# One graph layer's sums: the one-hot cast goes to GpSimd, five bins as pairs, ScalarE weighs five bins

## The chip, the cores and the metric

The kernel runs on one core of a Trainium2 chip. The metric is the device time in microseconds of one execution; three executions of the kernel before took 3258.47, 3259.68 and 3259.81 us, median 3259.68. The engines are TensorE (PE, with its weight loads as PEld), VectorE (DVE), ScalarE (ACT), GpSimd (POOL) and SyncE (SP), which issues the transfers.

## The reference

Two graph attention layers over 6250 nodes of 128 channels and 200000 edges, each followed by a residual and a layer norm. The change lies in the first:

```python
hij = concatenate([h[src], h[dst]], -1)
exp_e = exp(leaky_relu(hij @ w, 0.2) @ a)
denom = segment_sum(exp_e, src)
out = segment_sum(h[src] * exp_e / denom[src], dst)
x = layernorm(x + out)
```

What follows concerns the last two lines: rows of x divided by denom, gathered by source, weighed by exp_e, and summed by target.

## The kernel before, in words

Nodes stand in 49 blocks of 128 (node = block and lane). Earlier stages sort the edges into bins, one for each pair of a target block n and a source block b, at most 128 edges each, and leave for every bin the score of its edges (`e0`, one column of 128), the source lanes of its edges (in memory, `src_rows`) and the target lanes (`k.SL`). Then `layer0_sums` runs (from about 1318 to 2183 us of the profile). After it come `norm_and_project` and the second layer, `layer1`, which the change leaves alone, but which has instructions of the same kinds.

`layer0_sums` first divides x by denom and splits it into three bf16 parts (`parts`); VectorE and ScalarE share that work, which reaches into the first block's turns. The main loop has R = 343 turns, t = 0 to 342: seven turns for each target block n, and in each turn GX = 7 bins. A turn is made of these steps:

- SyncE fetches the source lanes, the same for all partitions (`got`, a ring of LOADS buffers).
- `make` (VectorE, L922): compares them with the partition's number: 128x896 bf16, seven one-hot matrices.
- `gather` (TensorE, L1009): 7 x 3 bf16 matmuls select the source rows into PSUM (`gps`, two buffers).
- `weigh` (VectorE, L930): the first SPLIT = 4 bins from PSUM times their scores, into `msg`.
- `weigh_late` (ScalarE, L1064): the other three bins, one instruction each, with the same result.
- `take_high` (ScalarE, L1070): copies the four bins, rounded to fp32r, into the first half of `halves`; `take_low` (VectorE, L936): subtracts that from the four bins and puts the remainder into the second half. A bin is then a pair of 128 columns that one fp32r matmul of 256 columns multiplies at once.
- `find_lanes` (VectorE, L847, a helper that other stages use too): one-hot matrices of the target lanes, 128x896 bf16 (`lane`).
- `widen` (ScalarE, L1055): casts them to fp32r (`lane_wide`).
- `add_up` (TensorE): the three late bins as full fp32 matmuls, two records each (L1020), then the four pairs (L1025), all into `acc`.

Once in seven turns, for the block that has been finished, VectorE's `take` adds the two halves of `acc` into S (a reduction, L941), GpSimd adds S to X (L995), and VectorE measures the rows for the layer norm (`measure` L946, `average` L950). ScalarE's `stage` lays out a block's target lanes.

The order on each queue is written out by hand. VectorE in turn t: make(t+2), weigh(t), find_lanes(t+1), take_low(t), and what is due for the block. ScalarE: weigh_late(t), take_high(t), widen(t+1). TensorE: gather(t+1), add_up(t). The rings `lane`, `lane_wide`, `msg` and `halves` have two buffers, `hot` has three.

Of the kernel before, what the change touches and what calls it, by code (L numbers as in the profile page):

```python
# [851 lines left out]
def layer0_sums(nc, k, parts, xs, den, src_rows, e0, X, S, mean_var):  # L852
    NB, PER = NBK, NBK // GX
    R = NB * PER
    RING, LOADS, SPLIT = 3, 4, 4
    BY_SCALAR = (2, 4, 6)
    F32R = mybir.dt.float32r
    with Stage(nc) as ctx:
        def sb(name, shape, dt=F32):
            return ctx.enter_context(nc.sbuf_tensor(f"l0_{name}", shape, dt))  # L860
# [11 lines left out]
        lane, lane_wide = sb("lane", [P, 2, GX, P], BF16), sb("lane_wide", [P, 2, GX, P], F32R)  # L872
        lane_pairs = sb("lane_pairs", [P, 2, NB, 2], BF16)
        msg, halves = sb("messages", [P, 2, GX, C]), sb("message_halves", [P, 2, SPLIT, 2, C], F32R)
        stats = sb("stats", [P, 2, 6])
        gps = ps("gathered", [P, 2, 1024])
        acc = ps("acc", [P, 2, 512])
# [11 lines left out]
        with nc.Block() as block:  # L889
# [10 lines left out]
            def _(dve):  # L900
# [24 lines left out]
                def weigh(t):  # L925
                    n, g = divmod(t, PER)
                    dve.wait_ge(s["gathered"], t + 1)
                    if t >= 2:
                        dve.wait_ge(s["low"], t - 1)
                    nc.vector.tensor_tensor(msg[:, t % 2, 0:SPLIT], gps[:, t % 2, 0:SPLIT * P].rearrange("p (i c) -> p i c", i=SPLIT),  # L930
                                            e0[:, n, g * GX:g * GX + SPLIT].unsqueeze(2).to_broadcast([P, SPLIT, C]), ALU.mult
                                            ).then_inc(s["messages"], 1)

                def take_low(t):
                    dve.wait_ge(s["high"], t + 1)
                    nc.vector.tensor_tensor(halves[:, t % 2, :, 1, :], msg[:, t % 2, 0:SPLIT], halves[:, t % 2, :, 0, :], ALU.subtract  # L936
                                            ).then_inc(s["low"], 1)

                def take(n):
                    dve.wait_ge(s["added"], (n + 1) * PER)  # L940
                    nc.vector.tensor_reduce(S[:, n, :], acc[:, n % 2, 0:2 * C].rearrange("p (q c) -> p c q", q=2), AX.X, ALU.add  # L941
                                            ).then_inc(s["taken"], 1)

                def measure(n):
                    dve.wait_ge(s["summed"], n + 1)
# [5 lines left out]

                def find_lanes(t):
                    n, g = divmod(t, PER)
                    if t >= 2:
                        dve.wait_ge(s["lane_wide"], t - 1)
                    if g == 0:
                        dve.wait_ge(s["staged"], n + 1)
                    compare_lanes(nc, k, lane[:, t % 2], lane_pairs[:, n % 2, g * GX:(g + 1) * GX, :]).then_inc(s["lane"], 1)

                ch.link(nc.vector.tensor_scalar(den, den, 1.1754944e-38, None, ALU.max))  # L960
                ch.link(nc.vector.reciprocal(rden[:], den))
                scale(0)
                scale(1)
                part_rest(0)
                for t in range(-2, R):
                    c = t + 3
                    if c + 1 < PER and c + 1 not in BY_SCALAR:
                        scale(c + 1)
                    if c < PER:
                        part_rest(c)  # L970
# [16 lines left out]
                take(NB - 1)  # L987
                measure(NB - 1)
                average(NB - 1)

            @block.gpsimd
            def _(pool):
                for n in range(NB):
                    pool.wait_ge(s["taken"], n + 1)
                    nc.gpsimd.tensor_tensor(X[:, n, :], X[:, n, :], S[:, n, :], ALU.add).then_inc(s["summed"], 1)  # L995

            @block.tensor
            def _(pe):
                def gather(t):
                    n, g = divmod(t, PER)  # L1000
# [12 lines left out]
                def add_up(t):  # L1013
                    n, g = divmod(t, PER)
                    pe.wait_ge(s["late_messages"], t + 1)
                    pe.wait_ge(s["lane_wide"], t + 1)
                    if g == 0 and n >= 2:
                        pe.wait_ge(s["taken"], n - 1)
                    for i in range(SPLIT, GX):
                        nc.tensor.matmul(acc[:, n % 2, 0:C], lane_wide[:, t % 2, i, :].bitcast(F32), msg[:, t % 2, i, :],  # L1020
                                         start=(g == 0 and i == SPLIT), stop=False, skip_group_check=True)
                    pe.wait_ge(s["low"], t + 1)
                    for i in range(SPLIT):
                        last = g == PER - 1 and i == SPLIT - 1
                        ins = nc.tensor.matmul(acc[:, n % 2, 0:2 * C], lane_wide[:, t % 2, i, :],  # L1025
                                               halves[:, t % 2, i].rearrange("p h c -> p (h c)"), start=False, stop=last,
                                               skip_group_check=True)
                    ins.then_inc(s["added"], 1)

                for t in range(-1, R):  # L1030
                    if t + 1 < R:
                        gather(t + 1)
                    if t >= 0:
                        add_up(t)

            @block.scalar
            def _(act):
# [13 lines left out]
                def widen(t):  # L1051
                    act.wait_ge(s["lane"], t + 1)
                    if t >= 2:
                        act.wait_ge(s["added"], t - 1)
                    nc.scalar.copy(lane_wide[:, t % 2], lane[:, t % 2]).then_inc(s["lane_wide"], 1)  # L1055

                def weigh_late(t):
                    n, g = divmod(t, PER)
                    act.wait_ge(s["gathered"], t + 1)
                    if t >= 2:  # L1060
                        act.wait_ge(s["added"], t - 1)
                    for i in range(SPLIT, GX):
                        b = g * GX + i
                        ins = nc.scalar.activation(msg[:, t % 2, i, :], gps[:, t % 2, i * P:(i + 1) * P], ACT.Copy,  # L1064
                                                   scale=e0[:, n, b:b + 1])
# [17 lines left out]
                part_middle(0)  # L1083
                part_high(2)
                part_middle(1)
                widen(0)
                for t in range(R):
                    c = t + 3
# [8 lines left out]
                    if t + 1 < R:  # L1097
                        widen(t + 1)
                    if t % PER == 3 and t // PER + 1 < NB:
                        stage(t // PER + 1)  # L1100

# [1424 lines left out]
```

## Time and profile before

The profiled execution spans 3274.5 us from the first to the last instruction, 14.8 us (0.45%) above the median of the times. The trace gives no other time of its own.

| | busy us | share of the span |
|---|---|---|
| PE | 3060.7 | 93% |
| PEld | 2792.8 | 85% |
| DVE | 3045.9 | 93% |
| ACT | 2750.1 | 84% |
| POOL | 155.0 | 5% |

An engine's busy time is the union of its instructions; neighbouring instructions of one engine overlap a little. The end of a matmul is modelled, so for TensorE the distance between starts is read. "Idle before" is the engine's idle time ahead of a group, with what ended it. A duration on GpSimd holds what the instruction waited for after its start.

### The profile page before, as it was taken

The page shows a single profiled execution, that of the slowest core. Times are in us where ns is not written, and L with a number is a line of the kernel's source. Part 1 is how long each engine was busy: PE and PEld are TensorE (multiplying, and loading weights), DVE is VectorE, ACT ScalarE, POOL GpSimd, SP SyncE. Part 2 cuts the span into 40 slices and gives each one's busy share as a digit, 9 for nine tenths or more (in the row PEclk, how much of TensorE's full clock was granted, in tenths as well). Part 3 has the DMA queues.
Part 4 walks back from the last instruction along what each step waited for, and adds up shares of the span by engine and source line. Part 5 has one row for each costly group of instructions (what it writes and reads, how often), then busy time and mean ns, then how long its engine had stood idle before and what let it go on. Part 6 is the DMA issues. An engine that isn't in the chain of part 4 may idle for free. (4 is left out here: it accounts for less than half of the span.)

```text
span 3274.5 us, 101508 instructions
## 1 busy us (share of the span) xinstructions
PE 3060.7 (93%) x40072; PEld 2792.8 (85%) x40072; DVE 3045.9 (93%) x4921; ACT 2750.1 (84%) x6946; POOL 155.0 (5%) x249
## 2 busy tenths in 40 slices
PE   5777699999999999699999999989999999999996
PEld 4666677778777877699999999988999999999994
DVE  8999889999999997799999999989999999999997
ACT  6988888888888885799999999987888888888887
POOL 0000000000000000000000000000111111111110
PEclk9989899999999997799999999999999999999998
DMA  3000022222222222234333333334455545554541
GB/s 66 13 14 11 23 98 93 87 93 94 93 87 93 94 86 48 65 96 97 97 97 96 97 96 97 97 93 137 161 163 160 164 161 163 161 163 161 162 151 41
DMA packets 173823, 333.06 MB, mean 102 GB/s; under 512 B 54876, under 2 KB 109616, under 8 KB 173264
## 3 DMA queue, kind: packets, MB, share of 16 engines
q1 hardware_dynamic: 170996, 323.30, 32.5%
q8 instruction: 322, 5.28, 0.7%
q10 hardware_dynamic: 2348, 3.20, 0.4%
q14 instruction: 157, 1.29, 0.1%
HBM read 320.77 MB, written 5.66 MB: 100 GB/s over the span
## 5 line engine op out<-in xcount | busy, mean ns | idle before, releaser
L1009 PE MATMUL l_gathered<-xp,l_src_onehot 128*128 128x128 bf16 x7203 | 467.0, 221 | 11.2 <-DVE l_src_onehot L922 11.2
L1436 PE MATMUL l_gathered<-hp,l_onehot 128*128 128x128 bf16 x7203 | 458.5, 219 | 0.0
L704 PE MATMUL sc_z<-sc_onehot,pq 128*128 128x256 f32 (+1 forms) x2450 | 429.4, 298 | 23.3 <-DVE sc_leaky L617 18.3
L1009 PEld LDWEIGHTS l_gathered<-xp,l_src_onehot 128*128 128x128 bf16 x7203 | 407.9, 99 | 26.3 <-DVE l_src_onehot L922 11.7
L788 ACT ACTIVATE sc_leaky<-sc_z 128x1024 f32<-128x1024 f32 (+3 forms) x325 | 309.8, 953 | 143.3 <-PE sc_z L708 140.5
L617 DVE SCALAR_TENSOR_TENSOR sc_leaky<-sc_z,sc_leaky 128x1024 f32<-128x1024 f32 (+3 forms) x325 | 370.1, 1139 | 60.0 <-ACT sc_leaky L788 52.5
L847 DVE TENSOR_TENSOR l_lane<-iota_b,l_lane_pairs 128x896 bf16<-128x896 bf16 x686 | 421.0, 614 | 0.0
L1436 PEld LDWEIGHTS l_gathered<-hp,l_onehot 128*128 128x128 bf16 x7203 | 406.1, 98 | 0.4
L708 PE MATMUL sc_z<-sc_onehot,pq 128*128 128x256 f32 (+1 forms) x2450 | 400.9, 286 | 0.0
L1450 PE MATMUL l_acc<-e,l_lane_wide 128*128 128x132 f32 x2744 | 385.5, 283 | 0.3 <-ACT e L1514 0.3
L704 PEld LDWEIGHTS sc_z<-sc_onehot,pq 128*128 128x128 f32 x2450 | 344.6, 196 | 35.9 <-issue 34.5
L708 PEld LDWEIGHTS sc_z<-sc_onehot,pq 128*128 128x128 f32 x2450 | 344.1, 195 | 0.0
L1343 DVE TENSOR_TENSOR e<-l_gathered,l_weight 128x768 f32<-128x768 f32 x343 | 325.5, 949 | 12.7 <-issue 9.1
L1450 PEld LDWEIGHTS l_acc<-e,l_lane_wide 128*128 128x128 f32 x2744 | 336.2, 190 | 0.8 <-ACT e L1514 0.5
L1503 ACT CAST l_lane_wide<-l_lane 128x896 fp32r<-128x896 bf16 x343 | 329.0, 959 | 0.0
L1055 ACT CAST l_lane_wide<-l_lane 128x896 fp32r<-128x896 bf16 x343 | 322.2, 939 | 4.0 <-DVE l_lane L847 4.0
L1508 ACT CAST l_message_halves<-e 128x396 fp32r<-128x396 f32 x343 | 179.1, 522 | 158.8 <-DVE e L1343 155.4
L1020 PE MATMUL l_acc<-l_messages,l_lane_wide 128*128 128x128 f32 x2058 | 306.0, 285 | 5.7 <-ACT l_messages L1064 5.7
L1064 ACT ACTIVATE l_messages<-l_gathered,e 128x128 f32<-128x128 f32 x1029 | 301.5, 363 | 0.0
L609 DVE TENSOR_SCALAR sc_onehot<-placed,part 128x1536 fp32r<-128x1536 uint8 (+1 forms) x300 | 298.9, 997 | 0.1
L936 DVE TENSOR_TENSOR l_message_halves<-l_messages,l_message_halves 128x512 fp32r<-128x512 f32 x343 | 237.5, 692 | 53.0 <-ACT l_message_halves L1070 48.2
L1514 ACT ACTIVATE e<-l_gathered,l_weight 128x32 f32<-128x32 f32 x1372 | 280.4, 286 | 0.0
(246 smaller groups left out, 6107.4 us busy)
## 6 DMA issues: line engine op xcount, KB each, us to landing
rows_got<-edge_rows_wide SPq DMA_DIRECT2D x338, 448.0 KB, 3.7
l_got<-edge_rows_src SPq DMA_DIRECT2D x343, 224.0 KB, 3.2
placed<-edge_rows SPq DMA_DIRECT2D x144, 512.0 KB, 3.7
out_dram<-X SPq DMA_DIRECT2D x12, 256.0 KB
S<-edge_rows_wide SPq DMA_DIRECT2D x5, 448.0 KB, 8.4
edge_rows<-e SPq DMA_DIRECT2D x98, 6.1 KB
edge_rows_wide<-e SPq DMA_DIRECT2D x98, 12.2 KB
sc_last_rows<-edge_rows SPq DMA_DIRECT2D x24, 64.0 KB, 3.5
```

Source lines behind the costliest of these rows:

```text
L617: nc.vector.scalar_tensor_tensor(out=y, in0=z, scalar=ALPHA, in1=y, op0=ALU.mult, op1=ALU.add).then_inc(s["leaky"], 1)
L704: nc.tensor.matmul(z[:, b, 0:nw, :], PQ[:, b0 + b, q, 0:C], hot[:, r % HOTS, b, 0, 0:nw, :], start=(b == u and q == 0), stop=False)
L708: ins = nc.tensor.matmul(z[:, u:u + v, n, :], PQ[:, 2 * pair + n, q, C:2 * C], hot[:, r % HOTS, u:u + v, 1, n, :], start=False, stop=(n == ...
L788: nc.scalar.activation(y, z, ACT.Relu, scale=1.0 - ALPHA).then_inc(s["positive"], 1)
L847: return nc.vector.tensor_tensor(out.rearrange("p i (u v) -> p i u v", v=2), k.iota_b[:].rearrange("p (u v) -> p u v", v=2).unsqueeze(1).t ...
L1009: ins = nc.tensor.matmul(gps[:, t % 2, i * P:(i + 1) * P], hot[:, t % RING, i, :], parts[:, g * GX + i, q, :], start=(q == 0), stop=(q == 2))
L1020: nc.tensor.matmul(acc[:, n % 2, 0:C], lane_wide[:, t % 2, i, :].bitcast(F32), msg[:, t % 2, i, :], start=(g == 0 and i == SPLIT), stop=Fa ...
L1055: nc.scalar.copy(lane_wide[:, t % 2], lane[:, t % 2]).then_inc(s["lane_wide"], 1)
L1343: nc.vector.tensor_tensor(msg[:, t % 2, 0:w, 0:C].rearrange("p i (e d) -> p i e d", e=HEADS), gps[:, t % 2, 0:w * P].rearrange("p (i e d) ...
L1436: ins = nc.tensor.matmul(gps[:, t % 2, i * P:(i + 1) * P], dst_hot[:, t % RING, i, :], hp[:, g * GX + i, q, 0:C], start=(q == 0), stop=(q ...
L1450: nc.tensor.matmul(acc[:, b % 2, 0:CW], lane_wide[:, t % 2, i, :].bitcast(F32), msg[:, t % 2, i, :], start=(g == 0 and i == SPLIT), stop=F ...
L1503: nc.scalar.copy(lane_wide[:, t % 2], lane[:, t % 2]).then_inc(s["lane_wide"], 1)
```

## The change

- `widen` moves from ScalarE to GpSimd, one 128x896 cast in each turn.
- `weigh` takes only BY_VECTOR = 2 bins; ScalarE's `weigh_late` takes five: bins 4, 5, 6, then, after a wait on the same turn's `weigh`, bins 2 and 3.
- SPLIT is 5: five bins are pairs (take_high, take_low and the fp32r matmuls), two bins stay full fp32 matmuls.
- The sums go straight to X: `take` adds the first half of `acc` to X on VectorE, a new `take_rest` the second half; GpSimd's addition and the detour over S are gone.
- `gather` runs two turns ahead of `add_up` instead of one, `take_low` comes one turn later than before in VectorE's order, right behind the next turn's `weigh`, and `make` and the first chunks of the preparation come one turn earlier. `take_high` waits on `late_messages` of its turn.
- The rings `lane`, `lane_wide`, `msg` and `halves` have KEPT = 3 buffers, `got` has 5.

```diff
-    RING, LOADS, SPLIT = 3, 4, 4
+    RING, LOADS, KEPT, SPLIT, BY_VECTOR, BANK = 4, 5, 3, 5, 2, 4
...
                 def weigh(t):
                     dve.wait_ge(s["gathered"], t + 1)
-                    if t >= 2:
-                        dve.wait_ge(s["low"], t - 1)
-                    nc.vector.tensor_tensor(msg[:, t % 2, 0:SPLIT], gps[:, t % 2, 0:SPLIT * P].rearrange("p (i c) -> p i c", i=SPLIT),
+                    if t >= KEPT:
+                        dve.wait_ge(s["low"], t - KEPT + 1)
+                    nc.vector.tensor_tensor(msg[:, t % KEPT, 0:BY_VECTOR], gps[:, t % 2, 0:BY_VECTOR * P].rearrange("p (i c) -> p i c", i=BY_VECTOR),
...
                 def take(n):
                     dve.wait_ge(s["added"], (n + 1) * PER)
-                    nc.vector.tensor_reduce(S[:, n, :], acc[:, n % 2, 0:2 * C].rearrange("p (q c) -> p c q", q=2), AX.X, ALU.add
-                                            ).then_inc(s["taken"], 1)
+                    nc.vector.tensor_tensor(X[:, n, :], X[:, n, :], acc[:, n % 2, 0:C], ALU.add).then_inc(s["taken"], 1)
+
+                def take_rest(n):
+                    dve.wait_ge(s["taken"], n + 1)
+                    nc.vector.tensor_tensor(X[:, n, :], X[:, n, :], acc[:, n % 2, C:2 * C], ALU.add).then_inc(s["summed"], 1)
...
-                for t in range(-2, R):
-                    c = t + 3
+                for t in range(-3, R + 1):
+                    c = t + 4
...
-                    if t + 2 < R:
-                        make(t + 2)
-                    if t >= 0:
+                    if t + 3 < R:
+                        make(t + 3)
+                    if 0 <= t < R:
                         weigh(t)
+                    if t >= 1:
+                        take_low(t - 1)
                     if 0 <= t + 1 < R:
                         find_lanes(t + 1)
-                    if t >= 0:
-                        take_low(t)
                     if t >= PER and t % PER == 2:
                         take(t // PER - 1)
+                    if t >= PER and t % PER == 3:
+                        take_rest(t // PER - 1)
...
             @block.gpsimd
             def _(pool):
-                for n in range(NB):
-                    pool.wait_ge(s["taken"], n + 1)
-                    nc.gpsimd.tensor_tensor(X[:, n, :], X[:, n, :], S[:, n, :], ALU.add).then_inc(s["summed"], 1)
+                def widen(t):
+                    pool.wait_ge(s["lane"], t + 1)
+                    if t >= KEPT:
+                        pool.wait_ge(s["added"], t - KEPT + 1)
+                    nc.gpsimd.tensor_copy(lane_wide[:, t % KEPT], lane[:, t % KEPT]).then_inc(s["lane_wide"], 1)
...
-                for t in range(-1, R):
-                    if t + 1 < R:
-                        gather(t + 1)
+                for t in range(-2, R):
+                    if t + 2 < R:
+                        gather(t + 2)
                     if t >= 0:
                         add_up(t)
...
                 def weigh_late(t):
                     act.wait_ge(s["gathered"], t + 1)
-                    for i in range(SPLIT, GX):
+                    for i in (*range(BANK, GX), *range(BY_VECTOR, BANK)):
+                        if i == BY_VECTOR:
+                            act.wait_ge(s["messages"], t + 1)
...
                 def take_high(t):
-                    act.wait_ge(s["messages"], t + 1)
-                    nc.scalar.copy(halves[:, t % 2, :, 0, :], msg[:, t % 2, 0:SPLIT]).then_inc(s["high"], 1)
+                    act.wait_ge(s["late_messages"], t + 1)
+                    nc.scalar.copy(halves[:, t % KEPT, :, 0, :], msg[:, t % KEPT, 0:SPLIT]).then_inc(s["high"], 1)
```

## Rows read from the trace of the kernel before

**Rows 1.** Busy time of each engine, 1400 to 2100 us; last: clock, DMA share, GB/s

```profile
1400.00:2100.00 700.00, 700.00 (x8953) 682.70 (x8951) 655.87 (x1279) 655.29 (x1486) 24.57 (x41) 1.00 0.35 97
```

**Rows 2.** Groups by line, 1400 to 2100 us: busy us, mean ns, idle before

```profile
L1055 ACT CAST l_lane_wide<-l_lane 128x896 fp32r<-128x896 bf16 x289 | 271.5, 939 | 0.0
...
L1064 ACT ACTIVATE l_messages<-l_gathered,e 128x128 f32<-128x128 f32 x867 | 254.0, 363 | 0.0
...
L936 DVE TENSOR_TENSOR l_message_halves<-l_messages,l_message_halves 128x512 fp32r<-128x512 f32 x289 | 200.1, 692 | 44.1 <-ACT l_message_halves L1070 39.9
...
L1070 ACT CAST l_message_halves<-l_messages 128x512 fp32r<-128x512 f32 x289 | 178.9, 619 | 44.9 <-DVE l_messages L930 29.5
...
L946 DVE BATCH_NORM_STATS2 l_stats<-X 128x6 f32<-128x128 f32 x41 | 11.8, 287 | 0.0
...
L950 DVE BATCH_NORM_AGGREGATE mean_var<-l_stats 128x2 f32<-128x6 f32 x41 | 7.1, 174 | 0.0
```

**Rows 3.** Timeline of one turn, TensorE and VectorE: start us, duration us

```profile
1706.74 0.68 DVE L930 TENSOR_TENSOR l_messages<-l_gathered,e 128x512 f32<-128x512 f32 x1
...
1707.10 1.35 PE L1009 MATMUL l_gathered<-xp,l_src_onehot 128*128 128x128 bf16 x21
1707.34 0.61 DVE L847 TENSOR_TENSOR l_lane<-iota_b,l_lane_pairs 128x896 bf16<-128x896 bf16 x1
...
1708.11 0.69 DVE L936 TENSOR_TENSOR l_message_halves<-l_messages,l_message_halves 128x512 fp32r<-128x512 f32 x1 [0.15 <-ACT l_message_halves L1070]
...
1708.28 0.89 PE L1020 MATMUL l_acc<-l_messages,l_lane_wide 128*128 128x128 f32 x6
1708.71 0.45 DVE L922 TENSOR_SCALAR l_src_onehot<-l_got,part 128x896 bf16<-128x896 bf16 x1
...
1708.92 0.71 PE L1025 MATMUL l_acc<-l_message_halves,l_lane_wide 128*128 128x256 f32 x4
1709.08 0.68 DVE L930 TENSOR_TENSOR l_messages<-l_gathered,e 128x512 f32<-128x512 f32 x1
...
1709.47 0.23 PE L1009 MATMUL l_gathered<-xp,l_src_onehot 128*128 128x128 bf16 x1
```

**Rows 4.** Timeline about one addition on GpSimd in this stage

```profile
1713.39 0.42 DVE L941 TENSOR_REDUCE S<-l_acc 128x128 f32<-128x256 f32 x1
1713.73 0.45 DVE L922 TENSOR_SCALAR l_src_onehot<-l_got,part 128x896 bf16<-128x896 bf16 x1
1713.89 0.60 POOL L995 TENSOR_TENSOR X<-X,S 128x128 f32<-128x128 f32 x1 [16.37 <-DVE S L941]
```

**Rows 5.** Timeline about GpSimd's three instructions in the second layer

```profile
2706.81 0.61 DVE L847 TENSOR_TENSOR l_lane<-iota_b,l_lane_pairs 128x896 bf16<-128x896 bf16 x1
...
2706.98 0.75 POOL L1390 TENSOR_TENSOR S<-S,l_low_sums 128x128 f32<-128x128 f32 x1 [10.89 <-ACT den L1524]
...
2707.48 0.69 DVE L1351 TENSOR_TENSOR l_message_halves<-e,l_message_halves 128x396 fp32r<-128x396 f32 x1
2707.70 0.52 POOL L1391 TENSOR_TENSOR den<-den,l_low_sums 128x4 f32<-128x4 f32 x1
...
2708.09 0.67 DVE L1298 TENSOR_SCALAR l_onehot<-rows_got,part 128x1792 bf16<-128x1792 bf16 x1
...
2708.20 0.98 POOL L1399 TENSOR_SCALAR X<-X 128x128 f32<-128x128 f32 x1
```

**Rows 6.** Two lines over the whole trace: duration ns min/median/max

```profile
L1351 DVE TENSOR_TENSOR l_message_halves<-e,l_message_halves x343: 552/571/687, 2239.6 to 3219.0; 128x396 fp32r<-128x396 f32 x172
L995 POOL TENSOR_TENSOR X<-X,S x49: 454/599/605, 1374.5 to 2182.4; 128x128 f32<-128x128 f32 x49
```

**Rows 7.** Groups of GpSimd, whole trace: busy us, mean ns, idle before

```profile
L2090 POOL IOTA iota_i<- 128x128 int32 x1 | 0.2, 244 | 0.6 <-POOLq L2515 0.6
L2091 POOL IOTA part_i<- 128x1 int32 x1 | 0.1, 136 | 0.0
```

More of the change, by code:

```diff
@@ L871, in layer0_sums @@
         hot = sb("src_onehot", [P, RING, GX, P], BF16)
-        lane, lane_wide = sb("lane", [P, 2, GX, P], BF16), sb("lane_wide", [P, 2, GX, P], F32R)
+        lane, lane_wide = sb("lane", [P, KEPT, GX, P], BF16), sb("lane_wide", [P, KEPT, GX, P], F32R)
         lane_pairs = sb("lane_pairs", [P, 2, NB, 2], BF16)
-        msg, halves = sb("messages", [P, 2, GX, C]), sb("message_halves", [P, 2, SPLIT, 2, C], F32R)
+        msg, halves = sb("messages", [P, KEPT, GX, C]), sb("message_halves", [P, KEPT, SPLIT, 2, C], F32R)
         stats = sb("stats", [P, 2, 6])
@@ L927, in weigh @@
                     dve.wait_ge(s["gathered"], t + 1)
-                    if t >= 2:
-                        dve.wait_ge(s["low"], t - 1)
-                    nc.vector.tensor_tensor(msg[:, t % 2, 0:SPLIT], gps[:, t % 2, 0:SPLIT * P].rearrange("p (i c) -> p i c", i=SPLIT),
-                                            e0[:, n, g * GX:g * GX + SPLIT].unsqueeze(2).to_broadcast([P, SPLIT, C]), ALU.mult
+                    if t >= KEPT:
+                        dve.wait_ge(s["low"], t - KEPT + 1)
+                    nc.vector.tensor_tensor(msg[:, t % KEPT, 0:BY_VECTOR], gps[:, t % 2, 0:BY_VECTOR * P].rearrange("p (i c) -> p i c", i=BY_VECTOR),
+                                            e0[:, n, g * GX:g * GX + BY_VECTOR].unsqueeze(2).to_broadcast([P, BY_VECTOR, C]), ALU.mult
                                             ).then_inc(s["messages"], 1)
@@ L935, in take_low @@
                     dve.wait_ge(s["high"], t + 1)
-                    nc.vector.tensor_tensor(halves[:, t % 2, :, 1, :], msg[:, t % 2, 0:SPLIT], halves[:, t % 2, :, 0, :], ALU.subtract
-                                            ).then_inc(s["low"], 1)
+                    nc.vector.tensor_tensor(halves[:, t % KEPT, :, 1, :], msg[:, t % KEPT, 0:SPLIT], halves[:, t % KEPT, :, 0, :],
+                                            ALU.subtract).then_inc(s["low"], 1)
                 def take(n):
                     dve.wait_ge(s["added"], (n + 1) * PER)
-                    nc.vector.tensor_reduce(S[:, n, :], acc[:, n % 2, 0:2 * C].rearrange("p (q c) -> p c q", q=2), AX.X, ALU.add
-                                            ).then_inc(s["taken"], 1)
+                    nc.vector.tensor_tensor(X[:, n, :], X[:, n, :], acc[:, n % 2, 0:C], ALU.add).then_inc(s["taken"], 1)
+                def take_rest(n):
+                    dve.wait_ge(s["taken"], n + 1)
+                    nc.vector.tensor_tensor(X[:, n, :], X[:, n, :], acc[:, n % 2, C:2 * C], ALU.add).then_inc(s["summed"], 1)
                 def measure(n):
@@ L953, in find_lanes @@
                     n, g = divmod(t, PER)
-                    if t >= 2:
-                        dve.wait_ge(s["lane_wide"], t - 1)
+                    if t >= KEPT:
+                        dve.wait_ge(s["lane_wide"], t - KEPT + 1)
                     if g == 0:
                         dve.wait_ge(s["staged"], n + 1)
-                    compare_lanes(nc, k, lane[:, t % 2], lane_pairs[:, n % 2, g * GX:(g + 1) * GX, :]).then_inc(s["lane"], 1)
+                    compare_lanes(nc, k, lane[:, t % KEPT], lane_pairs[:, n % 2, g * GX:(g + 1) * GX, :]).then_inc(s["lane"], 1)
                 ch.link(nc.vector.tensor_scalar(den, den, 1.1754944e-38, None, ALU.max))
@@ L987, in _ @@
                 take(NB - 1)
+                take_rest(NB - 1)
                 measure(NB - 1)
@@ L992, in _ @@
             def _(pool):
-                for n in range(NB):
-                    pool.wait_ge(s["taken"], n + 1)
-                    nc.gpsimd.tensor_tensor(X[:, n, :], X[:, n, :], S[:, n, :], ALU.add).then_inc(s["summed"], 1)
+                def widen(t):
+                    pool.wait_ge(s["lane"], t + 1)
+                    if t >= KEPT:
+                        pool.wait_ge(s["added"], t - KEPT + 1)
+                    nc.gpsimd.tensor_copy(lane_wide[:, t % KEPT], lane[:, t % KEPT]).then_inc(s["lane_wide"], 1)
+                for t in range(R):
+                    widen(t)
             @block.tensor
@@ L1017, in add_up @@
                     if g == 0 and n >= 2:
-                        pe.wait_ge(s["taken"], n - 1)
+                        pe.wait_ge(s["summed"], n - 1)
                     for i in range(SPLIT, GX):
-                        nc.tensor.matmul(acc[:, n % 2, 0:C], lane_wide[:, t % 2, i, :].bitcast(F32), msg[:, t % 2, i, :],
+                        nc.tensor.matmul(acc[:, n % 2, 0:C], lane_wide[:, t % KEPT, i, :].bitcast(F32), msg[:, t % KEPT, i, :],
                                          start=(g == 0 and i == SPLIT), stop=False, skip_group_check=True)
@@ L1024, in add_up @@
                         last = g == PER - 1 and i == SPLIT - 1
-                        ins = nc.tensor.matmul(acc[:, n % 2, 0:2 * C], lane_wide[:, t % 2, i, :],
-                                               halves[:, t % 2, i].rearrange("p h c -> p (h c)"), start=False, stop=last,
+                        ins = nc.tensor.matmul(acc[:, n % 2, 0:2 * C], lane_wide[:, t % KEPT, i, :],
+                                               halves[:, t % KEPT, i].rearrange("p h c -> p (h c)"), start=False, stop=last,
                                                skip_group_check=True)
                     ins.then_inc(s["added"], 1)
-                for t in range(-1, R):
-                    if t + 1 < R:
-                        gather(t + 1)
+                for t in range(-2, R):
+                    if t + 2 < R:
+                        gather(t + 2)
                     if t >= 0:
@@ L1049, in part_middle @@
                     nc.scalar.copy(parts[:, chunk(c), 1, :], xs[:, chunk(c), :]).then_inc(s["part_middle"], 1)
[L1051 to L1055, printed above, removed]
                 def weigh_late(t):
@@ L1059, in weigh_late @@
                     act.wait_ge(s["gathered"], t + 1)
-                    if t >= 2:
-                        act.wait_ge(s["added"], t - 1)
-                    for i in range(SPLIT, GX):
+                    if t >= KEPT:
+                        act.wait_ge(s["added"], t - KEPT + 1)
+                    for i in (*range(BANK, GX), *range(BY_VECTOR, BANK)):
+                        if i == BY_VECTOR:
+                            act.wait_ge(s["messages"], t + 1)
                         b = g * GX + i
-                        ins = nc.scalar.activation(msg[:, t % 2, i, :], gps[:, t % 2, i * P:(i + 1) * P], ACT.Copy,
+                        ins = nc.scalar.activation(msg[:, t % KEPT, i, :], gps[:, t % 2, i * P:(i + 1) * P], ACT.Copy,
                                                    scale=e0[:, n, b:b + 1])
@@ L1085, in _ @@
                 part_middle(1)
-                widen(0)
+                part_high(3)
+                part_middle(2)
                 for t in range(R):
-                    c = t + 3
+                    c = t + 4
                     if c < PER:
@@ L1096, in _ @@
                     take_high(t)
-                    if t + 1 < R:
-                        widen(t + 1)
                     if t % PER == 3 and t // PER + 1 < NB:
```

## The prediction

> **What bounds the kernel now.** I read first the busy time by stretch. From 1400 to 2100 us of the stage that the change touches, TensorE is busy all the time, VectorE 655.87 and ScalarE 655.29 of 700 us, at full TensorE clock [rows 1]. Three engines are within some 6% of each other, so the groups by line come next, for what the two that idle wait for. In those 700 us there are 289 casts, so a turn takes 700 / 289 = 2.42 us [rows 2], and there are 343 turns: each 0.01 us on a turn is 3.4 us of the kernel. All idle time of VectorE, 44.1 us or 0.15 us a turn, stands before take_low, which waits for ScalarE's take_high; all of ScalarE's, 44.9 us, stands before take_high, nearly all of it for VectorE's weigh [rows 2]. So the turn's length is set by a loop of two engines: weigh, take_high, take_low, make, next weigh. The timeline shows it: weigh at 1706.74, find_lanes 1707.34, a wait of 0.15, take_low 1708.11, make 1708.71, weigh 1709.08, 2.34 us in all [rows 3]; the block's own instructions make up the rest to 2.42.
>
> TensorE is right behind. By starts, gather takes 1707.10 to 1708.28 = 1.18, three full fp32 bins until 1708.92 = 0.64 (0.21 each), four pairs until 1709.47 = 0.55 (0.14 each): 2.37 us [rows 3]. Whatever the loop gives back, TensorE holds the turn at 2.37 as long as it has this work.
>
> **TensorE's part.** One bin becomes a pair: 0.14 instead of 0.21. The turn is 1.18 + 2 x 0.21 + 5 x 0.14 = 2.30. The most that the change can bring, if nothing else takes over, is (2.42 - 2.30) x 343 = 41 us.
>
> **ScalarE's part.** The cast (271.5 / 289 = 0.94 a turn) leaves. Weighing costs 254.0 / 867 = 0.29 for a bin, so five cost 1.46 for 0.88. take_high grows by 128 columns; the cast of 896 against 619 ns for 512 gives 0.83 ns a column, so 0.62 + 0.11 = 0.73 [rows 2]. Together 2.19 and a few hundredths for stage, below TensorE's 2.30. Additions two turns behind the gathers give the chain weigh, weigh_late, take_high, take_low a whole further turn, so ScalarE's new wait on weigh before bins 2 and 3 should hold up nobody but its own queue (take_high behind it), for which 0.1 us is left; gather(t+2) needs PSUM free of turn t, and by then TensorE has gather(t+1) and add_up(t-1) to do, some 2.3 us. I cost it at nothing; if that cover failed, it would be a few hundredths a turn.
>
> **VectorE's part, without GpSimd.** An instruction holds the engine for its duration less about 0.08, by starts: weigh 0.68 becomes 0.60, take_low 0.69 becomes 0.60, make 0.45 becomes 0.37 [rows 3]. Between take_low (692 ns, 512 columns [rows 2]) and the second layer's (571 ns, 396 columns [rows 6]) a column costs 1.04 ns. take_low of 640 columns is then 0.83, held 0.75; weigh of 256 columns 0.68 - 0.27 = 0.41, held 0.33; find_lanes is held 0.53; make 0.36. That is 1.97. A block adds take and take_rest, which no row shows: I take 0.29 for each as for measure, which reads as many columns (bounds: 0.17, average's, and 0.42, the old reduction's), and measure and average as before [rows 2, 4]. Held: 0.21 + 0.21 + 0.21 + 0.09 = 0.72, or 0.10 a turn. Sum 2.07, and the wait for take_high is gone, since it has a turn to spare. Alone, VectorE would be no bound.
>
> **The cast on GpSimd, and what it does to VectorE.** GpSimd has not been idle for nothing: the trace shows it and VectorE holding each other up. (a) In the second layer take_low takes 552 to 573 ns in nearly all turns, and 687 at most [rows 6]; the long ones stand where a GpSimd addition is under way. There, take_low starts at 2707.48 and runs 0.69 instead of 0.57, while GpSimd's addition ends at 2707.73 [rows 5]. The delay of 0.12 is GpSimd's end less the start of take_low (0.25) less 0.14. (b) That addition starts at 2706.98, but ends 0.31 after find_lanes ends (2707.42), 0.75 long; alone, the like addition of this stage takes 0.45 [rows 5, 6]. (c) The next addition, of 4 columns, ends (2708.22) 0.05 to 0.06 after take_low (2708.17). (d) The subtraction L1399 ends (2709.18) 0.41 after the second layer's make (2708.76) [rows 5]. (e) In this stage the addition starts at 1713.89, when make, from 1713.73, has begun, and ends 0.31 after make's end at 1714.18 [rows 4]. So find_lanes, take_low and make each exclude a GpSimd instruction that reads SBUF, and once GpSimd has begun, take_low is held until it ends. weigh, with one operand in PSUM, isn't longer beside them.
>
> How long must the cast, call it S, have this access to itself? No row shows one. Below: the two iotas give (244 - 136) / 127 = 0.85 ns a column [rows 7], and (c) shows 0.06 us after release for almost no columns, so S = 0.06 + 896 x 0.85 = 0.82. The subtraction, which like a cast has one input, took 0.41 for 128 columns; with the other 768 at 0.85, S = 1.07. I take the middle, 0.95. Far bounds: the addition's slope, (0.31 - 0.06) / 124 = 2.0 ns a column, gives 1.87; the subtraction's whole price per column, 3.2 ns, gives 2.89.
>
> Now the place. widen(t+1) is released by find_lanes(t+1), and GpSimd begins 0.08 after the releasing end [rows 4]. Next on VectorE is make, which starts 0.08 before find_lanes' end. Call that end 0. Make runs from -0.08 to 0.36; the cast gets in at 0.36 and ends at 0.36 + S. weigh starts at 0.28 and is hidden by it; take_low starts at 0.61 and is held for (0.36 + S) - 0.61 - 0.14 = S - 0.39, behind it find_lanes, on which the next cast waits. In three turns of seven (take, take_rest, measure) a further instruction of 0.2 us, which excludes nobody, stands between find_lanes and make. Then GpSimd is first: it gets in at 0.08 + 0.14 (0.45 alone less 0.31) = 0.22, and make, from 0.12, is held for (0.22 + S) - 0.12 - 0.14 = S - 0.04. Mean over seven: (4 (S - 0.39) + 3 (S - 0.04)) / 7 = S - 0.24. VectorE's turn is 2.07 + S - 0.24 = 1.83 + S.
>
> With S = 0.95 it is 2.78 us, against 2.42: 0.36 x 343 = +123 us. S = 0.82 gives 2.65 and +79, S = 1.07 gives 2.90 and +165. TensorE and ScalarE then wait for take_low, find_lanes and the cast. The changed start and end of the stage (a few instructions once, deeper rings, GpSimd's last addition gone) I put at no more than 4 us either way, hidden in the rest. On the profiled execution's 3274.5 us span that is 3397; on the median, which is 14.8 us lower, 3383.
>
> What the Trainium skill says beside this: "SBUF — State Buffer", section "Who interferes with whom", has VectorE instructions in a two-port mode contend with GpSimd both ways, whoever issues first blocking the other; the trace shows make blocking GpSimd (d, e), but not yet GpSimd blocking make, and by this page the sum stands as it is. "GPSIMD Engine Reference", section "Elementwise — side-by-side cycle accounting", puts the shortest one-input body at 1.03 cycles an element at 1.2 GHz and a good software loop at 1.8; as estimates S = 0.83 (+82 us) or 1.40 (+278 us). No row here decides between them.
>
> **The rivals.** (1) Faster: the cast holds up nothing that matters, because it needs the access only briefly. It decides from 1.83 + S = 2.42, S = 0.59, which is 0.6 ns a column all in. TensorE is then the bound: 2.30, -41 us, 3219. Against it: S would have to be under every price that the rows give, and VectorE's delay in (a) fits to the hundredth. Chance 0.13, for the chance that the cast isn't like those instructions. (2) make, once behind, isn't held by GpSimd, only take_low and find_lanes are. The three turns then cost (0.22 + S) - 0.81 - 0.14 = S - 0.73 each, the mean is S - 0.54, the turn 1.53 + S: 2.48 at S = 0.95, +21 us, 3281 (3236 to 3322 for S from 0.82 to 1.07). Nothing speaks for it but that no row shows it; chance 0.12. (3) GpSimd's cast is slow, as its additions are: S = 1.87, turn 3.70, +439 us, 3699; half way, S = 1.41, 3541. For it, L1399's 0.41 us for 128 columns; against it, the iota's slope. Chance 0.12.
>
> **How the numbers follow.** The forecast, 3383, has 0.63, and 3339 to 3425 as its own range. The range of all is 3240 to 3545: it holds the forecast, nearly all of (2), and the part of (3) up to half way; (1), at 0.13, and the far part of (3) are left out. A difference under 0.2%, 6.5 us, can't be told from none. Faster: (1) and a fifth of (2), 0.16; within it 0.03; slower 0.81.
>
> **What would show it.** Right: in the new profile take_low's mean is well above 0.83 us and make's has two values (about 0.45, and over 1.2 in three turns of seven), with weigh at 0.41; casts on GpSimd of 1.3 us or so in the record, beginning beside make; TensorE idle 0.4 us a turn; ScalarE near 80% busy. Wrong: take_low at 0.83 and make at 0.45 throughout, which is (1); or make always 0.45 and only take_low long, which is (2). A cast of over 2 us is (3).

## The result, and the profile after

The changed kernel takes 3302.46 us (3301.49 to 3302.98, four runs) against 3259.74: 1.0133 times as long, with an interval of 1.0118 to 1.0147, or 42.7 us more. The forecast was slower, 3383 us, 123 more. The direction and the mechanism stand; the extra time is a third of the one forecast, so the forecast of the size failed.

The changed kernel's busy times, 1400 to 2100 us (as [rows 1]):

```profile
1400.00:2100.00 700.00, 665.97 (x8147) 627.91 (x8144) 700.00 (x1240) 581.03 (x1667) 280.33 (x272) 1.00 0.32 91
```

VectorE has no gap left (655.87 before), TensorE has got some, ScalarE has dropped from 655.29 to 581.03: VectorE is now the bound. There are 271 find_lanes in the stretch, so a turn is 700 / 271 = 2.58 us instead of 2.42. The groups by line of the same stretch (as [rows 2]):

```profile
L936 DVE TENSOR_TENSOR l_message_halves<-l_messages,l_message_halves 128x640 fp32r<-128x640 f32 x272 | 282.2, 1038 | 0.0
L1003 POOL CAST l_lane_wide<-l_lane 128x896 fp32r<-128x896 bf16 x272 | 281.1, 1034 | 420.0 <-DVE l_lane L847 420.0
L1036 PE MATMUL l_acc<-l_message_halves,l_lane_wide 128*128 128x256 f32 x1355 | 232.8, 302 | 34.0 <-DVE l_message_halves L936 34.0
L922 DVE TENSOR_SCALAR l_src_onehot<-l_got,part 128x896 bf16<-128x896 bf16 x271 | 198.1, 731 | 0.0
...
L847 DVE TENSOR_TENSOR l_lane<-iota_b,l_lane_pairs 128x896 bf16<-128x896 bf16 x271 | 165.8, 612 | 0.0
...
L930 DVE TENSOR_TENSOR l_messages<-l_gathered,e 128x256 f32<-128x256 f32 x271 | 110.9, 409 | 0.0
...
L941 DVE TENSOR_TENSOR X<-X,l_acc 128x128 f32<-128x128 f32 x39 | 10.7, 274 | 0.0
```

weigh (409 ns) and find_lanes (612) are as long as their work. take_low means 1038 ns, make 731 instead of 442. All idle time of GpSimd ahead of its casts is for find_lanes, and all of TensorE's is for take_low. Where the excess stands is to be seen in the timeline, first a plain turn (one without an instruction of the block) up to the next find_lanes, then the turn with take (start us, duration us):

```profile
1705.48 0.61 DVE L847 TENSOR_TENSOR l_lane<-iota_b,l_lane_pairs 128x896 bf16<-128x896 bf16 x1
...
1706.01 0.44 DVE L922 TENSOR_SCALAR l_src_onehot<-l_got,part 128x896 bf16<-128x896 bf16 x1
1706.15 1.09 POOL L1003 CAST l_lane_wide<-l_lane 128x896 fp32r<-128x896 bf16 x1 [1.27 <-DVE l_lane L847]
...
1706.38 0.41 DVE L930 TENSOR_TENSOR l_messages<-l_gathered,e 128x256 f32<-128x256 f32 x1
1706.71 1.21 DVE L936 TENSOR_TENSOR l_message_halves<-l_messages,l_message_halves 128x640 fp32r<-128x640 f32 x1
...
1707.85 0.61 DVE L847 TENSOR_TENSOR l_lane<-iota_b,l_lane_pairs 128x896 bf16<-128x896 bf16 x1
...
1712.58 0.61 DVE L847 TENSOR_TENSOR l_lane<-iota_b,l_lane_pairs 128x896 bf16<-128x896 bf16 x1
...
1713.12 0.27 DVE L941 TENSOR_TENSOR X<-X,l_acc 128x128 f32<-128x128 f32 x1
1713.26 0.93 POOL L1003 CAST l_lane_wide<-l_lane 128x896 fp32r<-128x896 bf16 x1 [1.27 <-DVE l_lane L847]
1713.32 1.12 DVE L922 TENSOR_SCALAR l_src_onehot<-l_got,part 128x896 bf16<-128x896 bf16 x1
...
1714.36 0.41 DVE L930 TENSOR_TENSOR l_messages<-l_gathered,e 128x256 f32<-128x256 f32 x1
...
1714.69 0.81 DVE L936 TENSOR_TENSOR l_message_halves<-l_messages,l_message_halves 128x640 fp32r<-128x640 f32 x1
...
1715.42 0.61 DVE L847 TENSOR_TENSOR l_lane<-iota_b,l_lane_pairs 128x896 bf16<-128x896 bf16 x1
```

In the plain turn make is first (0.44, not held). The cast ends at 1707.24, 0.79 us after make's end at 1706.45: that is S, the time that the cast needs the access to itself. take_low takes 1.21 instead of 0.81, held 0.40. In the turn with take the cast is first and 0.93 long; make takes 1.12 instead of 0.44, held 0.68, and take_low its own 0.81. From find_lanes to find_lanes the plain turn is 2.37, the other 2.84.

The spans (3274.5 and 3300.5) don't compare directly: the profiled execution of the kernel before spent 17.5 us more ahead of this stage, at a lower TensorE clock (0.95 against 0.97, in code that is the same). So the stretches are compared: ahead of the stage, from its first division to the first weigh, the first block's seven turns, the other turns. First the kernel before, then the changed one (same columns as above; what follows is code that the change leaves alone):

```profile
0.00:1318.50 1318.50, 1172.27 (x13270) 963.72 (x13270) 1219.59 (x1552) 1066.03 (x2253) 0.53 (x6) 0.95 0.22 68
1318.50:1334.80 16.30, 5.63 (x45) 5.10 (x46) 12.39 (x16) 9.74 (x19) 0.00 (x0) 0.50 0.29 86
1334.80:1367.30 32.50, 22.32 (x192) 20.32 (x191) 23.68 (x37) 25.49 (x55) 0.00 (x0) 0.75 0.20 48
1367.30:2183.30 816.00, 814.22 (x10401) 793.70 (x10399) 762.61 (x1488) 761.08 (x1726) 29.21 (x49) 1.00 0.35 95
```

```profile
0.00:1301.00 1301.00, 1153.40 (x13270) 948.84 (x13270) 1219.07 (x1551) 1064.72 (x2253) 0.53 (x6) 0.97 0.22 69
1301.00:1319.30 18.30, 4.84 (x42) 4.32 (x42) 16.20 (x20) 13.10 (x27) 3.56 (x1) 0.50 0.36 102
1319.30:1345.00 25.70, 19.38 (x179) 18.38 (x180) 19.58 (x33) 20.78 (x54) 6.25 (x7) 0.73 0.22 60
1345.00:2212.50 867.50, 824.23 (x10071) 777.11 (x10070) 866.24 (x1536) 719.32 (x2062) 347.22 (x336) 1.00 0.31 89
```

The start costs 2.0 us more, the first block, whose turns share VectorE with the preparation, 6.8 less, and the other 336 turns 51.5 more: 46.7 in all, where the times differ by 42.7. Behind the stage, from 2183.3 and 2212.5 us on, the code is the same and the executions spend 1091.2 and 1088.0 us, 3.2 less after the change. That leaves 43.5; why the rest of the kernel was 3.2 us shorter is open.

### The profile page after: what moved, and what is told of

Its sections match the earlier page's. It is cut to its first block and busy times, and to the rows that moved or that the text cites. A ratio compares the mean times of both kernels' runs of the same rounds, so it can differ in the third digit from the quotient of the medians.

```text
span 3300.5 us, 101504 instructions
## 1 busy us (share of the span) xinstructions
PE 3045.7 (92%) x39729; PEld 2757.8 (84%) x39729; DVE 3148.9 (95%) x4970; ACT 2704.3 (82%) x7289; POOL 482.1 (15%) x543
## 5 line engine op out<-in xcount | busy, mean ns | idle before, releaser
L1003 POOL CAST l_lane_wide<-l_lane 128x896 fp32r<-128x896 bf16 x343 | 357.0, 1041 | 1850.6 <-DVE l_lane L847 1850.6
L1071 ACT ACTIVATE l_messages<-l_gathered,e 128x128 f32<-128x128 f32 x1715 | 509.2, 363 | 141.8 <-DVE l_messages L930 141.8
L704 PE MATMUL sc_z<-sc_onehot,pq 128*128 128x256 f32 (+1 forms) x2450 | 419.3, 293 | 23.6 <-DVE sc_leaky L617 18.5
L708 PE MATMUL sc_z<-sc_onehot,pq 128*128 128x256 f32 (+1 forms) x2450 | 393.7, 282 | 0.0
L704 PEld LDWEIGHTS sc_z<-sc_onehot,pq 128*128 128x128 f32 x2450 | 334.1, 191 | 35.9 <-issue 34.6
L936 DVE TENSOR_TENSOR l_message_halves<-l_messages,l_message_halves 128x640 fp32r<-128x640 f32 x343 | 356.7, 1040 | 0.3 <-ACT l_message_halves L1077 0.3
L1036 PE MATMUL l_acc<-l_message_halves,l_lane_wide 128*128 128x256 f32 x1715 | 295.7, 303 | 47.2 <-DVE l_message_halves L936 47.2
L708 PEld LDWEIGHTS sc_z<-sc_onehot,pq 128*128 128x128 f32 x2450 | 337.9, 192 | 0.0
L1509 ACT CAST l_lane_wide<-l_lane 128x896 fp32r<-128x896 bf16 x343 | 328.9, 959 | 0.0
L1036 PEld LDWEIGHTS l_acc<-l_message_halves,l_lane_wide 128*128 128x128 f32 x1715 | 225.6, 189 | 80.1 <-DVE l_message_halves L936 75.1
```

The lines of the kernel that those rows point to most:

```text
L704: nc.tensor.matmul(z[:, b, 0:nw, :], PQ[:, b0 + b, q, 0:C], hot[:, r % HOTS, b, 0, 0:nw, :], start=(b == u and q == 0), stop=False)
L708: ins = nc.tensor.matmul(z[:, u:u + v, n, :], PQ[:, 2 * pair + n, q, C:2 * C], hot[:, r % HOTS, u:u + v, 1, n, :], start=False, stop=(n == ...
L936: nc.vector.tensor_tensor(halves[:, t % KEPT, :, 1, :], msg[:, t % KEPT, 0:SPLIT], halves[:, t % KEPT, :, 0, :], ALU.subtract).then_inc(s[ ...
L1003: nc.gpsimd.tensor_copy(lane_wide[:, t % KEPT], lane[:, t % KEPT]).then_inc(s["lane_wide"], 1)
L1071: ins = nc.scalar.activation(msg[:, t % KEPT, i, :], gps[:, t % 2, i * P:(i + 1) * P], ACT.Copy, scale=e0[:, n, b:b + 1])
```

## The experiments

Each is against the kernel before, on the same chip (medians 3259.16 for the first four, 3257.70 for the others; 3259.74 stood against the changed kernel, so times from different groups compare to some 2 us). After a time stands its ratio to the kernel before, with the 95% interval. Theory A is the prediction's mechanism with the measured S = 0.79; theory B puts the loss on the new chain of waits, or says that the cast itself is cheap.

**Block's instructions beside the cast** (3230.78 us, ratio 0.991, 0.9892 to 0.9927)

```diff
                     if 0 <= t < R:
                         weigh(t)
+                    if PER <= t < R and t % PER == 2:
+                        take(t // PER - 1)
...
                     if 0 <= t + 1 < R:
                         find_lanes(t + 1)
-                    if t >= PER and t % PER == 2:
-                        take(t // PER - 1)
```

take_rest, measure and average move likewise.

> The changed kernel with one move in VectorE's order: take, take_rest, measure and average stand between weigh and take_low instead of between find_lanes and make. Nothing is added or left out. Theory A (VectorE is held while the cast has the SBUF access, 0.79 us from make's end on, and instructions with an operand in PSUM or only one in SBUF are not held): in every turn make is first and never held, take_low is held 0.40 us, and in the turns with an extra instruction only 0.2; the mean hold falls from 0.52 to about 0.30, the turn from 2.58 to 2.36 us, 76 us less than the changed kernel, near 3226 us. Theory B (the longer turn comes from the new chain of waits: gather two turns ahead, ScalarE's wait on weigh, take_high on late_messages): the same work in nearly the same order gives the same time, 3302 us within 7.

Same instructions, another order, 71.7 us less than the changed kernel (76 expected), and now 28 us faster than the kernel before. Its groups, 1400 to 2100 us, and the timeline with measure:

```profile
L936 DVE TENSOR_TENSOR l_message_halves<-l_messages,l_message_halves 128x640 fp32r<-128x640 f32 x297 | 330.5, 1113 | 0.0
L1003 POOL CAST l_lane_wide<-l_lane 128x896 fp32r<-128x896 bf16 x296 | 323.6, 1093 | 376.9 <-DVE l_lane L847 376.9
...
L922 DVE TENSOR_SCALAR l_src_onehot<-l_got,part 128x896 bf16<-128x896 bf16 x296 | 130.4, 441 | 0.0
```

```profile
1701.30 1.09 POOL L1003 CAST l_lane_wide<-l_lane 128x896 fp32r<-128x896 bf16 x1 [1.27 <-DVE l_lane L847]
1701.52 0.41 DVE L930 TENSOR_TENSOR l_messages<-l_gathered,e 128x256 f32<-128x256 f32 x1
1701.85 0.28 DVE L949 BATCH_NORM_STATS2 l_stats<-X 128x6 f32<-128x128 f32 x1
1702.05 1.01 DVE L936 TENSOR_TENSOR l_message_halves<-l_messages,l_message_halves 128x640 fp32r<-128x640 f32 x1
```

make is back at 441 ns; take_low is held by 0.20 behind measure and 0.40 in plain turns, as expected; the turn is 700 / 296 = 2.36, still VectorE's (700.00 us busy). Theory B is out as the cause of the loss: it had the same waits.

**One bin cast** (3203.78 us, ratio 0.9827, 0.9805 to 0.985) and **four bins cast** (a single execution, 3203.80 us)

```diff
-                    nc.gpsimd.tensor_copy(lane_wide[:, t % KEPT], lane[:, t % KEPT]).then_inc(s["lane_wide"], 1)
+                    nc.gpsimd.tensor_copy(lane_wide[:, t % KEPT, 0:1], lane[:, t % KEPT, 0:1]).then_inc(s["lane_wide"], 1)
```

The filling ahead of the loop isn't shown; with four bins, `0:4` stands for `0:1`.

> The changed kernel, but GpSimd casts only one of a turn's seven bins (128 columns); the other six hold matrices filled once before the loop, so six sevenths of the target lanes are left out and the output is not the reference's. All waits stay. Theory A: the cast has the access for about 0.16 us, take_low is never held (0.81 us throughout), make by up to 0.1 us in three turns of seven; VectorE's turn is about 2.1 us and TensorE is the bound at 2.30 to 2.32: about 3213 us. Theory B: the chain of waits is unchanged, so the time stays near 3302 us.

> As the run with one bin, with four of seven bins cast on GpSimd (512 columns), three left out. Theory A: the access is needed for 0.06 + 512 x 0.82 ns = 0.48 us; take_low is held 0.09 us (0.90 in four turns of seven), make 0.3 to 0.4 in the other three, the mean is 0.2, VectorE's turn 2.27, so the turn is 2.3 to 2.35 us, 3213 to 3225 us. Theory B: 3302 us.

With one bin, 1400 to 2100 us:

```profile
L936 DVE TENSOR_TENSOR l_message_halves<-l_messages,l_message_halves 128x640 fp32r<-128x640 f32 x308 | 250.9, 815 | 0.0
...
L922 DVE TENSOR_SCALAR l_src_onehot<-l_got,part 128x896 bf16<-128x896 bf16 x307 | 141.1, 460 | 0.0
L930 DVE TENSOR_TENSOR l_messages<-l_gathered,e 128x256 f32<-128x256 f32 x307 | 130.4, 425 | 36.6 <-PE l_gathered L1023 36.6
```

take_low is 815 ns, VectorE waits for TensorE's gather, and the turn is 700 / 307 = 2.28 us. That is TensorE's own limit with five pairs; the prediction had 2.30. Both times came out 9 us under the nearest that was expected, 3213. Four bins give the same turn, 2.28, with make held (592 ns in the mean) and take_low a little (843): below that limit a held VectorE costs nothing. The shortest cast of each run, which nothing has held, gives the price (duration ns min/median/max, for 128, 512 and 896 columns; the last is the changed kernel's):

```profile
L1003 POOL CAST l_lane_wide<-l_lane x343: 293/450/3022, 1314.6 to 2105.4; 128x128 fp32r<-128x128 bf16 x172
```

```profile
L1003 POOL CAST l_lane_wide<-l_lane x343: 616/773/3347, 1315.0 to 2108.7; 128x512 fp32r<-128x512 bf16 x172
```

```profile
L1003 POOL CAST l_lane_wide<-l_lane x343: 933/1091/3727, 1315.7 to 2208.0; 128x896 fp32r<-128x896 bf16 x172
```

A column costs (933 - 616) / 384 = 0.83 ns and (616 - 293) / 384 = 0.84 ns, the fixed part is 0.19 us. Of that, 0.93 - 0.79 = 0.14 comes before the access is taken.

**Writing only** (a single execution, 3243.87 us)

```diff
-                    nc.gpsimd.tensor_copy(lane_wide[:, t % KEPT], lane[:, t % KEPT]).then_inc(s["lane_wide"], 1)
+                    nc.gpsimd.memset(lane_wide[:, t % KEPT].bitcast(F32), 0.5).then_inc(s["lane_wide"], 1)
```

> The changed kernel with GpSimd's cast replaced by a memset of the same 896 fp32 columns with a constant, on the same waits: it only writes SBUF. The target lanes are left out, so the output is not the reference's. Theory A1 (what excludes take_low and find_lanes is only the second read; make needs more): take_low is 0.81 us throughout, make alone is held where GpSimd is first, three turns of seven, the turn is 2.32 to 2.4 us. Theory A2 (GpSimd's instruction holds everything with two SBUF inputs, whether it reads or not): as the changed kernel, take_low 1.2 us, 2.58 us a turn if the memset takes as long as the cast.

Its groups, 1400 to 2100 us:

```profile
L1003 POOL MEMSET l_lane_wide<- 128x896 f32 x291 | 276.6, 950 | 424.9 <-DVE l_lane L847 424.9
...
L936 DVE TENSOR_TENSOR l_message_halves<-l_messages,l_message_halves 128x640 fp32r<-128x640 f32 x290 | 234.2, 807 | 0.0
L922 DVE TENSOR_SCALAR l_src_onehot<-l_got,part 128x896 bf16<-128x896 bf16 x291 | 230.9, 794 | 0.0
```

A1 is right about who is held: beside a memset take_low never is (807 ns), make is, where it comes second. But that is four turns of seven and not three, since make is held in the turn with average too (the last section shows it), and the turn is 700 / 291 = 2.41, just above the 2.32 to 2.4 expected. So take_low and GpSimd meet over reading, make and GpSimd over writing too. "SBUF — State Buffer" of the Trainium skill, section "Who interferes with whom", says both: an instruction with two SBUF inputs contends with a GpSimd instruction that reads, one in a two-port mode with either, and the one that issues first has the access. This run and the changed kernel agree on who is held, with take_low at 807 ns beside a memset and 1.21 us beside a cast, and make at 1.03 and 1.12 us behind them. No run shows in which mode make runs.

**The cast alone** (3488.31 us, ratio 1.0724, 1.0698 to 1.075): the kernel before with ScalarE's widen removed, and

```diff
+                def widen(t):
+                    pool.wait_ge(s["lane"], t + 1)
+                    if t >= 2:
+                        pool.wait_ge(s["added"], t - 1)
+                    nc.gpsimd.tensor_copy(lane_wide[:, t % 2], lane[:, t % 2]).then_inc(s["lane_wide"], 1)
```

GpSimd's addition of S to X stands between the casts (not shown).

> The kernel before with one part of the change alone: GpSimd casts the lanes in each turn (rings of two, old order, three bins weighed by ScalarE, four pairs, GpSimd still adds S to X once a block, two turns later). Nothing is left out. Theory A: in the old order take_low comes right behind find_lanes and starts 0.15 us after its end (it waits for take_high), when the cast, started at 0.08, is already in; take_low is held until the cast ends at 0.22 + 0.79 = 1.01, that is for 1.01 - 0.15 - 0.14 = 0.72 us, in every turn. The turn is 2.42 + 0.72 = 3.14, +248 us, near 3507 us, with take_low at 1.4 us throughout. Theory B (the cast itself costs little, the rest of the change is what slows): 3260 us or less, since ScalarE loses 0.94 us a turn.

```profile
1702.14 0.61 DVE L847 TENSOR_TENSOR l_lane<-iota_b,l_lane_pairs 128x896 bf16<-128x896 bf16 x1
...
1702.82 0.94 POOL L997 CAST l_lane_wide<-l_lane 128x896 fp32r<-128x896 bf16 x1 [2.10 <-DVE l_lane L847]
1702.90 1.39 DVE L936 TENSOR_TENSOR l_message_halves<-l_messages,l_message_halves 128x512 fp32r<-128x512 f32 x1 [0.15 <-ACT l_message_halves L1074]
```

The timeline shows take_low at 1.39 instead of 0.69, and its mean over the 225 turns of the stretch is 1387 ns: it is held 0.70 in every turn. The turn is 700 / 225 = 3.11, and the cast in the old order costs 231 us (expected 248).

**All but the cast** (3239.19 us, ratio 0.9941, 0.9926 to 0.9957): SPLIT = BY_VECTOR = 4, take_high waits on messages, and on ScalarE's queue, right behind take_high, the cast:

```diff
-                    nc.gpsimd.tensor_copy(lane_wide[:, t % KEPT], lane[:, t % KEPT]).then_inc(s["lane_wide"], 1)
+                    nc.scalar.copy(lane_wide[:, t % KEPT], lane[:, t % KEPT]).then_inc(s["lane_wide"], 1)
```

> The changed kernel without the move of the cast and without the shift of bins: ScalarE casts the lanes and weighs three bins, VectorE four, four pairs; kept are the gathers two turns ahead, take_low one turn later, the rings of three, and the sums added to X by VectorE. Nothing is left out. Both theories are asked here whether the deeper pipeline is sound. Theory A: VectorE no longer waits for take_high; it needs 0.36 + 0.60 + 0.60 + 0.53 + 0.10 = 2.19, ScalarE about 2.2, TensorE 2.37 and is the bound: (2.37 - 2.42) x 343 = -17 us, and about 7 less from the first block, near 3236 us. Theory B (the new chain of waits slows): 3260 us or more, with VectorE or TensorE idle.

```profile
L930 DVE TENSOR_TENSOR l_messages<-l_gathered,e 128x512 f32<-128x512 f32 x295 | 203.9, 691 | 29.6 <-PE l_gathered L1013 24.3
L936 DVE TENSOR_TENSOR l_message_halves<-l_messages,l_message_halves 128x512 fp32r<-128x512 f32 x294 | 200.1, 681 | 0.0
```

No wait stands before take_low any more (44.1 us in [rows 2]); VectorE waits for gather instead, TensorE is the bound at 700 / 294 = 2.38 us. What it keeps of the change, the deeper pipeline and the sums that go straight to X, is worth 18.5 us; no run takes these two apart.

**Better versions.** The first experiment's order, with BY_VECTOR = 3 and ScalarE casting the last bins:

```diff
+                def widen_late(t):
+                    act.wait_ge(s["lane"], t + 1)
+                    if t >= KEPT:
+                        act.wait_ge(s["added"], t - KEPT + 1)
+                    nc.scalar.copy(lane_wide[:, t % KEPT, ON_POOL:], lane[:, t % KEPT, ON_POOL:]).then_inc(s["late_lanes"], 1)
```

TensorE and find_lanes wait for the late casts too (not shown); ON_POOL is 5 in the first version and 6 in the second.

> The run with the block's instructions beside the cast, and in addition: VectorE weighs three bins instead of two, and ScalarE casts two of the seven bins (after take_high of the same turn, with a semaphore of its own), GpSimd five. Nothing is left out. Theory A: the access is needed for 0.79 - 256 x 0.82 ns = 0.58 us, weigh is held 0.13 us longer under cover of it, so take_low is held (0.36 + 0.58) - 0.74 - 0.14 = 0.06 us in plain turns and not in the others; VectorE 2.06 + 0.13 + 0.04 = 2.23, ScalarE 2.16 - 0.26 + 0.38 = 2.28; TensorE is the bound at 2.28, as in the run with one bin: near 3204 us. Theory B (the order's gain had another cause than the hold): 3231 us or more, for VectorE's and ScalarE's instructions are longer.

> As the run with five bins cast on GpSimd, with six there and one on ScalarE. Theory A: the access is needed for 0.69 us, take_low is held 0.17 in plain turns and under 0.02 in three of seven, the mean is about 0.1; VectorE 2.06 + 0.13 + 0.1 = 2.29, ScalarE 2.18, TensorE 2.28: the turn is 2.28 to 2.30, near 3205 us. Theory B: 3231 us or more.

Five bins on GpSimd: 3205.46 us in a single execution. Six: 3203.75 us, ratio 0.9835 (0.9822 to 0.9848), 54 us less than the kernel before. Its groups, 1400 to 2100 us:

```profile
L1004 POOL CAST l_lane_wide<-l_lane 128x768 fp32r<-128x768 bf16 x307 | 303.3, 988 | 395.9 <-DVE l_lane L847 395.9
L936 DVE TENSOR_TENSOR l_message_halves<-l_messages,l_message_halves 128x640 fp32r<-128x640 f32 x308 | 274.1, 890 | 0.0
```

take_low is still held a little (890 ns), but the turn is 2.28, TensorE's, the same as with one bin cast. VectorE has no gap left either (700.00 us busy), so the two are level there; with five bins it has 12 us of 700.

## Why the prediction had the direction and not the size

- **What bounded the kernel before**: right. With the loop through take_high taken apart, TensorE holds the turn at 2.38 (2.37 had been read from its starts). One reading was too strong: of ScalarE's 44.9 us before take_high, the trace puts 29.5 down to weigh, two thirds and not nearly all; nothing in the sum hung on it.
- **TensorE's part**: 2.30 forecast, 2.28 measured. **ScalarE's part**: no bound, as forecast; 581 of 700 us busy. Its new wait on weigh was put at nothing, and with one bin cast, where all waits stay, the turn is indeed TensorE's.
- **VectorE without GpSimd**: 2.07 forecast. The durations where nothing is held, 0.81, 0.41, 0.61, 0.44 and 0.27 for take, are within 0.02 of those costed.
- **Who holds whom, and where**: right in each case of the changed kernel. The plain turn's hold is 0.40 where S - 0.39 gives 0.40; the three turns of seven have make held, which no row had shown, so rival 2 is out. There the formula S - 0.04 gives 0.75 and 0.68 was measured: 0.07 x 3 / 7 = 0.03 a turn, 10 us.
- **The step that failed** is the size of S, "I take the middle, 0.95". It is 0.79. The low end, 0.06 us and the iota's 0.85 ns a column, was nearly right (the cast: 0.83 to 0.84), and the high end took the subtraction's 0.41 us for 128 columns for a price of all one-input instructions, which it isn't: a cast of 128 columns takes 0.29 in all and has the access for 0.15. Of the prediction's two estimates beside its sum, 0.83 and 1.40, the first is near. 0.16 us a turn is 55 us of the 80 that the forecast was out. Another 10 are the formula's, above, 5 the start and the first block, 3 the stretch behind the stage; some 7 are left, 0.02 us a turn, which is as fine as the rows can be read. A price per column was to be had from one instruction of the same engine at two sizes; averaging it with another kind's single price made it worse.
- **The start** was put at 4 us either way; the first block gave back 6.8 us and the start cost 2.0.
- **The signs** came weaker than named, as a smaller S makes them: make at 1.12 where over 1.2 was named, casts of 1.03 us in the mean for 1.3, and TensorE idle for 34.0 / 271 = 0.13 us a turn for 0.4.
- The range, 3240 to 3545, held the 3302 us; the likeliest case's own, from 3339, did not. Rival 1 needed S under 0.59, and the runs with less cast show that threshold from the other side: at one and at four bins (S about 0.15 and 0.48) nothing is lost. The chance of faster, 0.13 and a fifth of 0.12, adds up to 0.15, not 0.16.

What the change does has then three parts, each with a run that shows it: the deeper pipeline, with the sums straight to X, frees some 18 us; the fifth pair takes TensorE's limit from 2.38 to 2.28; the cast on GpSimd keeps VectorE at 2.58, above both.

## What to carry to other kernels

Work moved to an idle GpSimd was paid by VectorE here wherever their SBUF access collided: price it as the time that GpSimd has the access, minus what VectorE does meanwhile with instructions that aren't held. Here these were weigh, take and take_rest, with one operand in PSUM, and measure and average, with one fp32 operand in SBUF. A single operand in SBUF is not enough: make, which compares bf16 columns with a per-partition scalar, is held. So where work must go to GpSimd, let one held instruction that is due anyway come first, as make does here, and put the others beside GpSimd's; the order alone was worth 72 us. Take the price of an instruction from the same engine's rows at two sizes, and don't mix it with the fixed cost of another kind.

## What the runs showed of the hardware

A GpSimd instruction that only writes doesn't hold a VectorE tensor_tensor with two SBUF inputs (807 ns beside 896 columns of memset), but it holds the bf16 comparison with a per-partition scalar (1.03 us in place of 0.44 where the memset was first), and is held by it:

```profile
1701.50 0.44 DVE L922 TENSOR_SCALAR l_src_onehot<-l_got,part 128x896 bf16<-128x896 bf16 x1
1701.64 1.09 POOL L1003 MEMSET l_lane_wide<- 128x896 f32 x1 [0.87 <-DVE l_lane L847]
...
1703.60 0.84 POOL L1003 MEMSET l_lane_wide<- 128x896 f32 x1 [0.87 <-DVE l_lane L847]
1703.66 1.03 DVE L922 TENSOR_SCALAR l_src_onehot<-l_got,part 128x896 bf16<-128x896 bf16 x1
```

In this timeline of the run that only writes, the memset takes 0.84 where it is first and 1.09 where make is.

Which one is first isn't decided by the recorded start alone. In the turn with average, make starts 0.04 to 0.05 us ahead of GpSimd; beside the memset it is held all the same, beside the changed kernel's cast (the last two lines) it isn't:

```profile
1711.78 1.13 DVE L922 TENSOR_SCALAR l_src_onehot<-l_got,part 128x896 bf16<-128x896 bf16 x1
1711.82 0.84 POOL L1003 MEMSET l_lane_wide<- 128x896 f32 x1 [1.90 <-DVE l_lane L847]
...
1721.73 0.42 DVE L922 TENSOR_SCALAR l_src_onehot<-l_got,part 128x896 bf16<-128x896 bf16 x1
1721.78 1.16 POOL L1003 CAST l_lane_wide<-l_lane 128x896 fp32r<-128x896 bf16 x1 [1.91 <-DVE l_lane L847]
```

An estimate from the rows fits: where make is first, the memset ends at 1702.73, 0.79 us after make (1701.94), so of its 0.84 us alone only 0.05 come before it has the access, against the cast's 0.14.
